# Shared expert's second layer: three products of 256 columns instead of 512 + 256, and one closing operation per tile

## What is computed

```python
x_flat = x.reshape(-1, H)                       # 2048 x 256, after the second layernorm
top_w, sel = top_k(softmax(x_flat @ gate_w.T), 2)
h  = gelu(einsum('th,ehf->tef', x_flat, W1) + b1)     # 8 experts, f = 1024
y  = einsum('tef,efh->teh', h, W2) + b2
out = einsum('teh,te->th', y, combine)
sh = gelu(x_flat @ sW1 + sb1)                   # the shared expert, 256 -> 1024 -> 256
out = out + sh @ sW2 + sb2
x  = x + tanh(g_ffn[0]) * out
```

## Time and profile before

| | before |
|---|---|
| median of 3 runs | 581.27 us (579.91 to 586.54) |
| the profiled execution, in all | 582.31 us |
| its span, first to last instruction | 580.6 us |
| TensorE products busy | 529.0 us (91%), 3115 instructions |
| TensorE weight loads busy | 459.2 us (79%), 3116 |
| VectorE busy | 327.6 us (56%), 697 |
| ScalarE busy | 242.9 us (42%) |
| GpSimd busy | 292.6 us (50%) |
| mean granted TensorE clock | 0.943 |

### The profile page before, as it was taken

The page is one execution under the profiler, slowest core; times in us unless marked ns, Lnnn a source line. Parts: engine busy times, 40 slices in busy tenths (PEclk is TensorE's granted clock), DMA queues, the critical chain, the costliest instruction groups (busy, mean ns, idle before and its releaser), DMA issues.

```text
span 580.6 us, 11601 instructions
## 1 busy us (share of the span) xinstructions
PE 529.0 (91%) x3115; PEld 459.2 (79%) x3116; DVE 327.6 (56%) x697; ACT 242.9 (42%) x524; POOL 292.6 (50%) x266
## 2 busy tenths in 40 slices
PE   4799899999999799749999999999999999999983
PEld 3489799998997677627888888888888888888772
DVE  3334867666574455515556655556565556643758
ACT  2211657766675335304343344343344334334440
POOL 7130666889758167753044435334344436005770
PEclk9775989999899699959999999999999999999998
DMA  5733445666689422256256666666666654102452
GB/s 144 187 99 119 106 132 147 180 171 198 197 277 307 156 73 104 104 189 181 75 174 192 227 181 206 192 209 190 217 198 224 192 181 117 36 19 77 142 151 76
DMA packets 59676, 92.13 MB, mean 159 GB/s; under 512 B 6413, under 2 KB 45565, under 8 KB 59653
## 3 DMA queue, kind: packets, MB, share of 16 engines
q0 software_dynamic: 24544, 56.77, 33.2%
q1 hardware_dynamic: 26597, 27.67, 15.0%
q10 hardware_dynamic: 8512, 7.40, 4.2%
HBM read 67.10 MB, written 20.71 MB: 151 GB/s over the span
## 4 chain that ended last, share of the span: by engine, by line
PE 69%; DMA 7%; POOL 7%; DVE 5%; issue 5%; ACT 4%; ACTq 1%; SPq 1%; DVEq 0%; POOLq 0%
PE ps L784 13%; PE ps L771 7%; PE ps L785 6%; PE ps L773 6%; PE ps L772 6%; PE ps L757 6%; POOL routed_x L632 5%; PE ps L731 3%; PE ps L851 3%; PE ps L833 3%; PE ps L895 2%; PE ps L881 2%; DMA x<-x2row 2%; DMA moved_q<-hid 2%; PE ps L748 2%
## 5 line engine op out<-in xcount | busy, mean ns | idle before, releaser
L784 PE MATMUL ps<-w2hl,hTh 128*128 x312 | 114.8, 407 | 0.0
L1241 ACT ACTIVATE hid<-hid 128x512 f32<-128x512 f32 x78 | 49.3, 632 | 96.8 <-DVE hid L1431 96.8
L785 PE MATMUL ps<-w2hl,hTl 128*128 x312 | 87.7, 281 | 0.0
L1431 DVE TENSOR_TENSOR hid<-ps,b1bc 128x512 f32<-128x512 f32 x78 | 53.8, 691 | 30.2 <-PE ps L773 25.0
L1235 ACT ACTIVATE hTh<-ps 128x512 fp32r<-128x512 f32 x78 | 42.5, 596 | 65.5 <-PE ps L757 65.5
L784 PEld LDWEIGHTS ps<-w2hl,hTh 128*128 128x128 f32 x312 | 58.7, 188 | 12.6 <-issue 0.3
L771 PE MATMUL ps<-w1l,xT 128*128 x156 | 66.0, 423 | 1.5 <-DVE xT L1419 1.5
L524 POOL TENSOR_TENSOR w2hl<-stage,w2hl 128x2048 f32 (+1 forms) x8 | 36.9, 4613 | 51.6 <-DMA w2hl<-in_L_ffn_W 46.9
L773 PE MATMUL ps<-w1h,xT 128*128 x156 | 62.5, 400 | 0.0
L772 PE MATMUL ps<-w1h,xT 128*128 x156 | 62.4, 400 | 0.0
L785 PEld LDWEIGHTS ps<-w2hl,hTl 128*128 128x128 f32 x312 | 59.1, 189 | 0.0
(11 more groups left out here) (200 smaller groups left out, 1150.7 us busy)
## 6 DMA issues: line engine op xcount, KB each, us to landing
stage<-in_L_ffn_W POOLq DMA_DIRECT2D x14, 1024.0 KB, 6.2
w1h<-in_L_ffn_W POOLq DMA_DIRECT2D x7, 1024.0 KB, 5.5
w2hl<-in_L_ffn_W POOLq DMA_DIRECT2D x7, 1024.0 KB, 8.1
qstack<-moved_q SPq DMA_DIRECT2D x48, 128.0 KB, 2.6
xrow<-routed_x SPq DMA_DIRECT2D x39, 128.0 KB, 2.2
routed_y<-yrow ACTq DMA_DIRECT2D x39, 128.0 KB, 1.7
routed_x<-zeros SPq DMA_DIRECT2D x6, 768.0 KB, 6.7
moved_q<-hid SPq DMA_DIRECT2D x16, 256.0 KB, 3.7
```

The costliest lines, as they stand in the source:

```text
L784: mm(p_y, hTh[:, c, :], part(2 * D), start=c == 0, stop=False)
L785: last = mm(p_y[:, 0:D], hTl[:, c, :], part(D), start=False, stop=c == FC - 1)
L1241: act.activation(hid[:, n, :], hid[:, n, :], ACT.Gelu).then_inc(S["h_act"], 1)
L1431: tt(hid[:, n, :], p_h[:, n, :], b1bc[:, bass.ds(s, 1), n * (F // 2):(n + 1) * (F // 2)].rearrange("p o f -> p (o f)"), ALU.add).then_inc( ...
```

## The change

In `wide_down`, the 512-column product is split into two of 256: hi with the lo columns, and hi with the hi columns, and both go into columns 0 to 255 of the bank, where the third product goes too. The bank then holds the whole sum of a tile, and `wide_result` is one operation, which signals `sh_sum` directly; the semaphore `sh_mid` is dropped. For the last block (w = 3, token tiles 12 to 15) the bias, times the gate, is added to the residual tile early, by a new `last_bias` behind `wide_rest(25)`; the end is then one operation per tile, `last_result`, which reads the bank, multiplies by the gate and adds to `xres`. `combine` waits for `y_added` for all tiles.

```diff
-                    mm(ps[:, b, :], half_of(hTh, g)[:, at], w2hl[:, s, m, :], start=m == 0, stop=False)
-                    last = mm(ps[:, b, 0:D], half_of(hTl, g)[:, at], w2hl[:, s, m, 0:D],
-                              start=False, stop=m == FC - 1)
+                    hi, lo = half_of(hTh, g)[:, at], half_of(hTl, g)[:, at]
+                    mm(ps[:, b, 0:D], hi, w2hl[:, s, m, D:2 * D], start=m == 0, stop=False)
+                    mm(ps[:, b, 0:D], hi, w2hl[:, s, m, 0:D], start=False, stop=False)
+                    last = mm(ps[:, b, 0:D], lo, w2hl[:, s, m, 0:D], start=False, stop=m == FC - 1)
...
-                tt(ywide[:, j, :], ps[:, py_banks[j], 0:D], b2bc[:, s, :], ALU.add).then_inc(S["sh_mid"], 1)
-                dve.wait_ge(S["sh_mid"], n + 1)
-                tt(ywide[:, j, :], ps[:, py_banks[j], D:2 * D], ywide[:, j, :], ALU.add).then_inc(S["sh_sum"], 1)
+                tt(ywide[:, j, :], ps[:, py_banks[j], 0:D], b2bc[:, s, :], ALU.add).then_inc(S["sh_sum"], 1)
...
-                if w == NW - 1:
-                    dve.wait_ge(S["g_done"], j + 1)
                 stt(xres[:, t, :], ywide[:, j, :], tgate[:, 1:2], xres[:, t, :], ALU.mult, ALU.add
-                    ).then_inc(S["out_ready" if w == NW - 1 else "y_added"], 1)
+                    ).then_inc(S["y_added"], 1)
+
+            def last_bias(t):
+                dve.wait_ge(S["w2_ready"], PH)
+                stt(xres[:, t, :], b2bc[:, (PH - 1) % 2, :], tgate[:, 1:2], xres[:, t, :], ALU.mult, ALU.add
+                    ).then_inc(S["y_added"], 1)
+
+            def last_result(j):
+                t = (NW - 1) * WIDE_T + j
+                dve.wait_ge(S["sh_y"], t + 1)
+                dve.wait_ge(S["g_done"], j + 1)
+                stt(xres[:, t, :], ps[:, py_banks[j], 0:D], tgate[:, 1:2], xres[:, t, :], ALU.mult, ALU.add
+                    ).then_inc(S["out_ready"], 1)
...
             def combine(t):
                 dve.wait_ge(g_in[t // 2], 16 * 2 * TOP)
-                if t < NT - WIDE_T:
-                    dve.wait_ge(S["y_added"], t + 1)
+                dve.wait_ge(S["y_added"], t + 1)
...
+                if g == G1 + FC + 1:
+                    for t in range(NT - WIDE_T, NT):
+                        last_bias(t)
                 for t in COMBINED.get(g - G1, ()):
                     combine(t)
             combine(14)
             combine(15)
             for j in range(WIDE_T):
-                wide_result(NW - 1, j)
-                wide_add(NW - 1, j)
+                last_result(j)
```

More of the change, by code:

```diff
@@ L273, in gated_cross_attention_and_moe @@
             xT_ps xT_hi xT_lo h_ps h_add h_act hT_ps hT_hi hT_lo y_ps y_mid y_sum y_done y_stored
-            wx_ps wx_hi wx_lo sh_ps sh_act sh_hi sh_lo sh_down sh_y sh_mid sh_sum y_added
+            wx_ps wx_hi wx_lo sh_ps sh_act sh_hi sh_lo sh_down sh_y sh_sum y_added
             sb1_in g_mid g_done out_ready out_stored""".split()
```

## The result

Over 15 runs of each kernel in turn the changed kernel has a median of 578.19 us (573.70 to 583.76), the kernel before 582.85 (579.91 to 587.80). The ratio is 0.990 with a 95% interval of 0.987 to 0.993: 1.0% faster, 5.9 us (4.0 to 7.7). The ratio leaves out two executions of the changed kernel (582.95 and 583.76 us) that were in a slower state; the plain medians, with them, differ by 4.7 us. In a second set of runs the ratio was 0.990 again (0.986 to 0.994). The forecast was 4.8 us, which lies inside the interval of 4.0 to 7.7, so the times alone don't say that anything was missing from the sum. The traces do: of the stretch that the change touches, most executions of the kernel before took 1.5 us more than the one that I had summed from.

A forecast was written before the change was run, and what follows sets the result against it. The tail was taken as TensorE-bound except a mid-tail gap and the end, where VectorE is busy. Terms -1.33 - 3.6 + 0.1 = -4.8 us gave a 576.5 us median; bounds 576.3 to 578.2, with scatter 574 to 580.5.

The forecast's parts named there:

- The weight load: In wide_down, a third load per tile hides under products of 256 columns: 0 us, at most 0.22 us per tile.
- The boundary: VectorE at group 24: three results of one operation each let wide_down(25) start earlier, -1.33 us, bounds 0 and -1.4.
- The hole: TensorE's recorded wait ahead of wide_down(25), 2.07 us in the kernel before, was to shrink by some 0.4.
- The biases: Four added VectorE operations between the rests of groups 25 and 26, covered by 0.6 us: 0 us, bounds 0 and +1.65.
- The end: After the last combines, VectorE's twelve operations become four, 5.33 us to 1.72: -3.6 us, at least 3.2 gained.
- The stores: Last four tiles' stores, 0.41 us apart instead of 1.31, overlap and cost +0.1 us, bounds 0 and +1.2.
- so SP keeps up: On SP's queue, a store issue takes 0.33 us, so issuing follows the last tiles at 0.41 us apart.
- everything between them goes at TensorE's pace: In the tail, only a mid-tail gap of about 2.4 us and the last 9.30 us aren't bound by TensorE.
- 1 (the load shows): In wide_down, loads no longer hide under three short products: up to 14 us slower, about 590 us; chance 0.05.
- 2 (biases not covered): At group 25, added biases show or TensorE's wait stays, so only the end gains: 577.8 us; chance 0.13.
- 3 (the end turns to the DMA): At the end, stores pile up or the last gather is awaited, losing 0.5 to 1.2 us: about 577.4; chance 0.12.
- 4: Whole kernel: no change, 581 us, if another engine ends as late as VectorE did; chance 0.03.

The follow-up runs named there:

- products alone: Kernel before with only its products changed to three of 256 columns per tile, VectorE's work unchanged; 0.9999 of the kernel before, interval 0.997 to 1.003.
- four products: Changed kernel with the hi x hi product cut into two of 128 columns; group period 3.23 us, 56.16 us from group 16 to the end.
- the spread order: Changed kernel with VectorE's early biases, adds and combines moved to other groups; 50.14 us from group 16 to the end, no TensorE wait ahead of group 25.
- the end undone: Changed kernel without the early bias, two VectorE operations per last tile instead of one; 52.68 us from group 16 to the end.

## Why the prediction came out as it did

**The weight load** was costed at 0, and it is. Twice: the ratio of products alone is 0.9999, and its stretch is 57.4 against 57.2 for the kernel before with the same clock, so 0.2 us for 64 tiles, 3 ns for each added product. My bound from the earlier trace rows, 0.11 us for a load under 0.116, is what four products then measured. By the 2.5 ns for each product at full clock of the Trainium skill's "TensorE: Matmul & The Clock Gate", section "Back-to-back issue gap", the 64 added products come to 0.16 us, an estimate that these 0.2 us bear out. The section gives that figure for isolated products and says that a stream is spaced otherwise. I had left it out of the sum as too small for the rows.

**The boundary** was costed at -1.33 us, and it is -1.33 (28.37 to 27.04), and a second operation put back undid it. The hole itself shrank by 0.57 us where I had named 0.4: TensorE reaches group 24 0.12 us later than before (22.57 behind group 16, not 22.45), by its 2.81 us for a group.

**The biases** at 0: they are hidden, with 0.8 us to spare where I had found 0.6; one place earlier they cost 1.6.

**The end** at -3.6: it is -3.68 (5.33 to 1.65). **The stores** at +0.1: they are +0.28 (2.15 to 2.43), within the bounds that I had kept. The step that failed in this term is "so SP keeps up": an issue took 0.33 us by itself, 0.45 in a row of four, and the 0.3 us are lost on SP's queue and not in the transfers: the last issue began 0.21 us behind VectorE's last operation instead of 0.03, and took 0.45 instead of 0.33.

**The sum** was -4.8 us and the same two executions show -4.66 behind group 16. In the executions as they are on the mean it is more: 57.19, 57.28, 57.19 and 55.72 for the kernel before have a mean of 56.85, against 51.1. That is 5.7 us; the times say 5.9, with an interval (4.0 to 7.7) that holds 4.7 as well. That the profiled pair came out so near to my sum is luck: with any other of the four executions of the kernel before it would have been 6.1 to 6.2 us.

**What failed** is the sentence with which the prediction begins its search: that between the hole and the end "everything between them goes at TensorE's pace". TensorE's pace is not one pace. I priced the hole at its idle time alone, from one execution in which the clock behind it happened to stay up. In seven of eight executions with a recorded hole of 2.0 us or more (1.99 to 3.09), the granted clock behind it fell, and groups 25 and 26 took 1.5 us more. In the three with a hole of 1.5 us it didn't, nor in the three with a shorter one or none. So the change gained, by these executions, about 1.5 us in most of its runs on top of the 1.33. Whether the shorter hole did that, or the two short waits for banks that went with it, isn't shown: seven of the eight had these waits ahead of the hole, the eighth (3.09 us) had not, and no run has a hole of 2.0 us without them. It is an unpriced term of the sum, with the sign that helped; the range held it because it was drawn for the scatter of the runs. The Trainium skill describes something near to it in "TensorE: Matmul & The Clock Gate", section "HAM oscillation": waits between bursts of products send the clock to half, and the next burst starts slow. It tells this of waits that are longer than the 2.0 us here and that come again and again; in these traces it is one hole, and the fall comes after the products had started again.

**The rivals.** 1 (the load shows): no, but it would have been true at 128 columns. 2 (biases not covered): no. 3 (the end turns to the DMA): 0.18 us of it is true; with 1.8 us more off TensorE's end it is the whole truth, as the spread order showed. 4: no.

**The bounds** that I summed to -3.1 to -5.0 us don't add up to that. With the bounds as each term had them (0 for the boundary, +1.65 for the biases, -3.2 for the end, +1.2 for the stores) the small end of the gain is 0.35 us and not 3.1. The measured gain of 5.7 to 5.9 us lies beyond the large end, 5.0, by the missing term, so the wrong small end wasn't tested.

**Chances.** Faster by over 1% was given 0.15 and the ratio is 0.990, on the line. I had let it hang on the scatter or an undersized term, and not on a term that was missing.

What stays open: whether the clock falls in the changed kernel in some executions (it didn't in two, nor in the one with the end undone, which has the same hole), whether the length of the hole or the two waits ahead of it decide, and what made the one execution of the kernel before escape.

## What to carry to other kernels

Before a wait of TensorE is costed by its length, look at the granted clock of the stretch behind it, and in more than one execution: the same 2 us wait of the kernel before cost 2 us in one execution and 3.5 us in three. A product may be cut along its columns, so that sums fall into one place and the engine behind has less to do, as long as the pieces cover a weight load (here 256 columns did and 128 did not). When the tail of the engine that ends last is cut, look for what lands just before it: here it was the last gather, which became the bound with the next 1.8 us.

## What the hardware showed that I had not expected

- A wait of TensorE of 2.0 us, with two shorter ones ahead of it, was followed in six of seven executions by a lower granted clock (0.64 on the mean of the next 4.8 us) that began 0.4 to 1.3 us after the products had started again; at 1.5 us and no shorter ones this didn't happen in three executions.
- A weight load of 128x128 has a record of 0.19 us, but loads beside products of 128 columns started 0.11 us apart: that was the pace of those products.
- SP issued a store of 128 KB in 0.33 us by itself, and four in a row in 1.80 us, 0.45 each, while issue to landing stayed at 1.7 to 1.8 us.
